# Expert stage: spare rows in four buffers, asked for three quads ahead, and a later start for the weights of experts 6 and up

## What is computed

```python
C = int(math.ceil(CAPACITY_FACTOR * T / E))          # 1.25 * 4096 / 32 = 160
top1 = jnp.argmax(probs, axis=-1)
pos = jnp.cumsum(onehot, axis=0)[jnp.arange(T), top1] - 1
accepted = pos < C
buf = jnp.zeros((E * C + 1, H)).at[slot].set(xt)
g = jnp.einsum('ech,ehf->ecf', buf, w_gate)
u = jnp.einsum('ech,ehf->ecf', buf, w_up)
y = jnp.einsum('ecf,efh->ech', jax.nn.silu(g) * u, w_down)
return (xt + out_tok).reshape(B, S, H)               # out_tok: the token's row of y, times its gate
```

## Time and profile before

| | us |
|---|---|
| median of 3 runs | 3612.1 |
| these runs | 3604.91 to 3613.67 |
| the profiled execution's own time | 3612.02 |
| its span in the profile | 3610.2 |

### The profile page before, as it was taken

One profiled execution on the slowest core, in us unless ns is written; L12 is line 12 of the kernel. 1 busy time (PEld: TensorE's weight loads), 2 busy tenths in 40 slices (PEclk: granted clock), 3 DMA queues, 4 the chain that ended last, 5 costly groups with the idle time before them and its releaser, 6 DMA issues. The chain is left out here.

```text
span 3610.2 us, 52197 instructions
## 1 busy us (share of the span) xinstructions
PE 3197.4 (89%) x18048; PEld 1971.1 (55%) x18048; DVE 2459.1 (68%) x4614; ACT 1846.4 (51%) x3942; POOL 1413.2 (39%) x967
## 2 busy tenths in 40 slices
PE   8599999979999799899999899898388888887867
PEld 5244444346666555566666555333255556555766
DVE  8488887657767622277777332498799999996623
ACT  2176776836666511166666211356477777774100
POOL 4201111132222211132222211234699999996612
PEclk9699999989999899999999899999699999999888
DMA  5945576010020033000200131244615151512874
GB/s 168 164 63 90 78 97 125 28 38 24 23 62 25 29 151 98 26 23 23 63 25 19 56 96 47 72 152 149 241 59 205 59 205 59 204 59 73 294 232 143
DMA packets 263747, 347.27 MB, mean 96 GB/s; under 512 B 70620, under 2 KB 183242, under 8 KB 262845
## 3 DMA queue, kind: packets, MB, share of 16 engines
q1 hardware_dynamic: 249572, 308.29, 30.7%
q10 hardware_dynamic: 9432, 23.35, 2.0%
q0 software_dynamic: 4480, 12.30, 0.9%
HBM read 227.72 MB, written 112.80 MB: 94 GB/s over the span
## 5 line engine op out<-in xcount | busy, mean ns | idle before, releaser
L2411 POOL TENSOR_TENSOR H_feed<-H_ndu,H_bs 128x1024 f32<-128x1024 f32 x256 | 595.1, 2367 | 5.3 <-DMA H_cs<-between_bc 3.1
L888 ACT ACTIVATE B_probs<-B_p_exp,B_key_bias 128x512 f32<-128x512 f32 (+3 forms) x768 | 394.1, 582 | 159.7 <-PE B_p_exp L950 129.2
L779 DVE TENSOR_REDUCE B_part_max<-B_p_max 128x1 f32<-128x512 f32 (+3 forms) x768 | 374.5, 545 | 78.7 <-PE B_p_max L914 76.2
L1298 ACT ACTIVATE D_probs<-D_scores,D_neg,D_rq 128x256 f32<-128x256 f32 x512 | 282.9, 574 | 255.4 <-DVE D_neg L1219 255.4
L2382 ACT ACTIVATE H_decay<-H_ndt,H_rate 128x1024 f32<-128x1024 f32 x256 | 287.7, 1125 | 199.0 <-DVE H_turning L2464 103.3
L1662 PE MATMUL E_p_ag<-E_hT,FA_w 128*128 128x512 f32 x640 | 284.1, 603 | 1.9 <-ACT E_hT L1618 1.9
L911 PE MATMUL B_p_max<-B_k,B_q 100*128 100x512 bf16 (+3 forms) x768 | 256.3, 340 | 30.0 <-DMA B_q<-in_q_rows 20.1
L947 PE MATMUL B_p_exp<-B_q,B_k 100*128 100x512 bf16 (+3 forms) x768 | 249.6, 329 | 23.1 <-DMA B_q<-B_shift_rows 16.2
L2464 DVE TENSOR_TENSOR_SCAN H_turning<-H_decay,H_feed 128x1024 f32<-128x1024 f32 x112 | 253.5, 2274 | 20.2 <-POOL H_feed L2411 17.4
L2515 PEld LDWEIGHTS H_p_y<-H_minus,H_sT 128*128 128x128 f32 x1792 | 222.4, 198 | 75.9 <-ACT H_sT L2367 56.1
L2515 PE MATMUL H_p_y<-H_minus,H_sT 128*128 128x128 f32 x1792 | 230.9, 285 | 35.7 <-ACT H_sT L2367 35.7
(11 more groups left out here) (276 smaller groups left out, 6812.3 us busy)
## 6 DMA issues: line engine op xcount, KB each, us to landing
H_bs<-between_bc SPq DMA_DIRECT2D x64, 512.0 KB, 7.3
H_cs<-between_bc SPq DMA_DIRECT2D x36, 512.0 KB, 7.6
B_q<-between_q_parts SPq DMA_DIRECT2D x90, 128.0 KB
B_k<-between_k_parts SPq DMA_DIRECT2D x90, 128.0 KB
between_slots_x<-E_clear ACTq DMA_DIRECT2D x4, 2570.0 KB, 18.8
I_xe<-between_slots_x ACTq DMA_DIRECT2D x32, 257.0 KB, 3.0
LA_base<-between_z SPq DMA_DIRECT2D x64, 128.0 KB, 2.2
between_z<-D_z SPq DMA_DIRECT2D x64, 128.0 KB
```

The costliest lines, as they stand in the source:

```text
L779: nc.vector.reduce_max(part_max[:, g % 2, kc, qb, h:h + 1], p_max[:, use % 3, 0:keys], AX.X).then_inc(maxed, 1)
L888: nc.scalar.activation(probs[:, x % PROBS, skip:512], p_exp[:, n % SCORES, skip:512], ACT.Exp, bias=key_bias[:, g % SETS, kb - 4 * Q + 4, ...
L1298: last = nc.scalar.activation(probs[:, place[m], :, :].rearrange("p a b -> p (a b)"), scores[:, place[m], :, :].rearrange("p a b -> p (a b ...
L2411: nc.gpsimd.tensor_tensor(feed[:, n % AHEAD, :], ndu[:, g % 2, :], bs[:, s, :], ALU.mult).then_inc(fed, 1)
```

## The change

`xr`, `token_rest` and the semaphores `xr_loaded` get four buffers. ACT asks for the spare rows of quads 1, 2 and 3 right after the first six experts' rows, and from then on for those of quad `e // QUAD + 3` at the second expert of a quad; the last such request is that for quad 7 at expert 17. `tokens_rest(f)` waits for the return of quad f - 4, since that one used the same list. SP gets seven waits ahead of the weights of expert 6: for the spare rows of quad 0 and for the rows of experts 0 to 5. The order of the work on PE and DVE stays as it is.

```diff
-        QUAD, HR = 4, 8
+        QUAD, HR, XR = 4, 8, 4
-        token_rest = a.sb("token_rest", [P, 2, 1], I32)
+        token_rest = a.sb("token_rest", [P, XR, 1], I32)
-        xr = a.sb("xr", [P, 2, ROW])
+        xr = a.sb("xr", [P, XR, ROW])
-        xr_loaded = [a.sem(f"xr_loaded_{b}") for b in range(2)]
+        xr_loaded = [a.sem(f"xr_loaded_{b}") for b in range(XR)]
@@ SP @@
             for c in range(K - 2, K):
                 store_sums(c)
+            sp.wait_ge(xr_loaded[0], 16 * QUAD)
+            for b in range(XE - 2):
+                sp.wait_ge(xe_loaded[b], 16)
             for e in range(K - 2, EXPERTS):
                 load_weights(e)
@@ DVE @@
             def tokens_rest(f):
-                dve.wait_ge(xr_loaded[f % 2], 16 * QUAD * (f // 2 + 1))
-                reached(dve, rest_returned[f % 2], 16 * (f // 2))
-                nc.vector.tensor_scalar(token_rest[:, f % 2, :], xr[:, f % 2, TOKEN:TOKEN + 1], -1.0, float(TOKENS),
+                dve.wait_ge(xr_loaded[f % XR], 16 * QUAD * (f // XR + 1))
+                if f >= XR:
+                    dve.wait_ge(rest_returned[f % 2], 16 * ((f - XR) // 2 + 1))
+                nc.vector.tensor_scalar(token_rest[:, f % XR, :], xr[:, f % XR, TOKEN:TOKEN + 1], -1.0, float(TOKENS),
@@ ACT @@
             def load_rests(f):
-                if f >= 2:
-                    act.wait_ge(xe_turned, (f - 2) * QUAD + 1)
-                    act.wait_ge(y_ready, rest_use(f - 2) + 1)
-                    act.wait_ge(rest_tokens_ready, f - 1)
+                if f >= XR:
+                    act.wait_ge(xe_turned, (f - XR) * QUAD + 1)
+                    act.wait_ge(y_ready, rest_use(f - XR) + 1)
+                    act.wait_ge(rest_tokens_ready, f - XR + 1)
...
-            load_rests(1)
+            for f in range(1, XR):
+                load_rests(f)
...
-                if e % QUAD == 1 and QUAD <= e < EXPERTS - QUAD:
-                    load_rests(e // QUAD + 1)
+                if e % QUAD == 1 and QUAD <= e < EXPERTS - (XR - 1) * QUAD:
+                    load_rests(e // QUAD + XR - 1)
```

More of the change, by code:

```diff
@@ L2764, in _ @@
                     pool.wait_ge(rest_tokens_ready, f + 1)
-                    pool.indirect_dma_start(T["out"][:, :], bass.IndirectOffsetOnAxis(token_rest[:, f % 2, :], axis=0),
+                    pool.indirect_dma_start(T["out"][:, :], bass.IndirectOffsetOnAxis(token_rest[:, f % XR, :], axis=0),
                                             y_rest[:, f % 2, :], None, bounds_check=TOKENS - 1, oob_is_err=False
@@ L2878, in put_y_rest @@
                 reached(dve, rest_returned[f % 2], 16 * (f // 2))
-                nc.vector.scalar_tensor_tensor(y_rest[:, f % 2, :], p_y[:, rest_use(f) % 2, :], xr[:, f % 2, GATE:GATE + 1],
-                                               xr[:, f % 2, SUM], ALU.mult, ALU.add).then_inc(y_ready, 1)
+                nc.vector.scalar_tensor_tensor(y_rest[:, f % 2, :], p_y[:, rest_use(f) % 2, :], xr[:, f % XR, GATE:GATE + 1],
+                                               xr[:, f % XR, SUM], ALU.mult, ALU.add).then_inc(y_ready, 1)
             def tokens(e):
@@ L2938, in load_rests @@
             def load_rests(f):
-                if f >= 2:
-                    act.wait_ge(xe_turned, (f - 2) * QUAD + 1)
-                    act.wait_ge(y_ready, rest_use(f - 2) + 1)
-                    act.wait_ge(rest_tokens_ready, f - 1)
+                if f >= XR:
+                    act.wait_ge(xe_turned, (f - XR) * QUAD + 1)
+                    act.wait_ge(y_ready, rest_use(f - XR) + 1)
+                    act.wait_ge(rest_tokens_ready, f - XR + 1)
                 for j in range(QUAD):
                     at = (f * QUAD + j) * CAPACITY + P
-                    act.dma_start(xr[REST * j:REST * j + REST, f % 2, :], T["slots_x"][at:at + REST, :]
-                                  ).then_inc(xr_loaded[f % 2], 16)
+                    act.dma_start(xr[REST * j:REST * j + REST, f % XR, :], T["slots_x"][at:at + REST, :]
+                                  ).then_inc(xr_loaded[f % XR], 16)
             def put_xT(c):
@@ L3026, in turn_rows @@
                 if e % QUAD == 0:
-                    pe.wait_ge(xr_loaded[f % 2], 16 * QUAD * (f // 2 + 1))
+                    pe.wait_ge(xr_loaded[f % XR], 16 * QUAD * (f // XR + 1))
                     for k in range(KD):
                         nc.tensor.transpose(p_xr[:, k, :, :].rearrange("p j n -> p (j n)"),
-                                            xr[:, f % 2, k:DIM:KD], ident[:, :])
+                                            xr[:, f % XR, k:DIM:KD], ident[:, :])
                 for k in range(KD):
```

## The result

| | before | after |
|---|---|---|
| median of 5 runs, us | 3610.99 | 3572.2 |
| these runs | 3604.91 to 3613.67 | 3567.76 to 3576.65 |
| the profiled execution's own time | 3612.02 | 3574.62 |
| its span | 3610.2 | 3572.8 |

The ratio is 0.9892, 95% interval 0.9882 to 0.9903: 38.8 us less, against 40.8 forecast (3571.2, range 3562 to 3588).

A forecast was written before the change was run, and what follows sets the result against it. The prediction took PE to bound the stage of experts, interrupted by the late `xr` transfer. From 3612.0 us it took 36.4 for the advance and 4.4 for the hold, giving 3571.2 us, range 3562 to 3588.

The forecast's parts named there:

- What bounds the stage: Stage of experts: PE bounds it, interrupted by the `xr` transfer asked for one loop pass before it is read.
- rival D: Stage of experts: PE's stall has another cause, earlier requests move only the label; time 3608, chance 0.03.
- (1) Advance: -36.4: Six quad periods: three quads of advance remove the stalls, 123.15 us falls to 86.8, and nothing is late next.
- (2) DMA capacity: Stage of experts: DMA work exceeds PE's 14.46 us a quad, piling up about 1 us for each of five quads.
- rival B: Stage of experts: DMA engines become the bound if bytes take some 3% longer; time 3576 to 3586, chance 0.18.
- The rule set against a row: DMA rate: the skill's 358 GB/s gives 14.1 us for a period's bytes, the row 15.9; the prediction took the row.
- (3) The hold: -4.4: Stage start: with weights of experts 6 to 11 held, the last scatter lands in 3.2 us, 4.4 earlier (0 to 5.3).
- (4) ACT's requests: Before the first Silu: eight more DMAs slip it 2.0 us within 3.7 us of slack; cost 0, up to 1.5.
- Sum: Whole kernel: 3612.0 - 36.4 - 4.4 = 3571.2 us; bounds of the parts give 3570.3 to 3577.1.
- C: DVE's `tokens(e)`: the return of `y` takes the stall's place if landings exceed 10 us; 3583 to 3601, chance 0.10.
- E: Stage of experts: slower than before through DMA load, needing a rate of 225 GB/s; 3638 at 0.6, chance 0.03.
- weights landed in more than 13 us: Sign in the changed profile: weights land in over 13 us at DMA share near 1, PE never waiting for them.

The follow-up runs named there:

- no_late_weights: Kernel before without loading the weights of experts 12 to 31, which use what lies in the ring (wrong results): 3578.15 us, ratio 0.9908.
- burst_behind_rows: Kernel before plus SP's seven waits, each burst of weights for a quad also waiting until the previous quad's spare rows landed: 3582.98 us, ratio 0.9921.
- buffers_only: Changed kernel without SP's seven waits, four buffers and three quads of advance kept: 3580.58 us, ratio 0.9904.
- extra_one: Changed kernel plus one 256 KB DRAM to DRAM DMA behind each expert's weights from expert 6 on: 3565.4 us, ratio 0.9874.
- hold_until_scattered: Changed kernel with SP waiting for the scatters of the routing instead of the rows: 3572.09 us, ratio 0.9887.
- hold_only: Kernel before plus SP's seven waits alone, two buffers for the spare rows: 3606.61 us, ratio 0.9987.
- extra_two: Changed kernel plus two 256 KB DRAM to DRAM DMAs behind each expert's weights from expert 6 on: 3586.76 us, ratio 0.9936.
- three_warm_short: Changed kernel with three buffers, quad 2's request behind the first Silu and 13 matmuls without use on PE before the first transposes: 3570.57 us, ratio 0.9882.

## Why the prediction was right, step by step

- **What bounds the stage.** PE, interrupted by the transfer of `xr`: right. But the price was put on lateness alone, although rival D cites the last period, in which no weights are asked for and there is no stall. no_late_weights shows that the late request costs 2.9 us of the 36.1 by itself, and with burst_behind_rows that the burst of weights beside it is what lengthens the landing until PE also loses its clock.
- **(1) Advance: -36.4.** The free quad of 14.46 us measured 14.50 to 14.51. The six periods went from 123.15 to 87.03 us, 36.1 less; buffers_only gives 37.5 for the stage. The term is right to 1 us. That nothing is late next holds as well.
- **(2) DMA capacity.** This is the step with a wrong size. It set 15.1 to 15.9 us of DMA work (length times share) for a quad against 14.46 us, and so found a pile of 5 us, 9 with the held weights. In the kernel after the share falls to 0.99 in the fourth window, which a growing pile would not allow, and the engines caught up soon after the last request for weights, which is at 3527.30 (after, columns as above):

```profile
3536.00:3538.00 2.00, 2.00 (x17) 1.97 (x16) 0.23 (x1) 0.44 (x1) 1.58 (x2) 1.00 0.51 107
3538.00:3542.00 4.00, 4.00 (x28) 3.85 (x27) 2.16 (x8) 0.44 (x1) 0.98 (x1) 1.00 0.24 87
```

  Two sizes were off. The share of engines that never rest is 1.04 or 1.05 and not 1, so a window of 14.5 us can hold 15.2 us of such work. And GB/s over share went from 318 to 332 in the four rows of before to 333 to 369 after, and 358 to 375 in extra_one. Gaps are not what made the rate of before low; inside its bursts, with the engines full, it is some 320 GB/s too:

```profile
3509.00:3519.00 10.00, 4.93 (x32) 4.63 (x32) 1.92 (x6) 0.63 (x2) 1.97 (x2) 0.94 1.01 325
3530.50:3540.50 10.00, 5.10 (x32) 4.71 (x31) 2.10 (x7) 0.44 (x1) 1.70 (x2) 0.88 1.01 323
```

  Why the kernel after moves more bytes for the same share stays open. Nothing of the sum hung on this step, but the point at which rival B begins did: by the prediction at 3% less rate; in fact one extra DMA for each expert, a third more weight traffic, was still free.
- **The rule set against a row.** The prediction set the Trainium skill's figure from "DMA: Bandwidth & Descriptors", section Specifications, about 358 GB/s as the HBM limit of a core, against the row with 235 GB/s over a share of 0.74, and went by the row. By that figure nothing would pile up, which came nearer to what happened than my pile did. It is not a ceiling here, though: windows of 387 (after) and 394 GB/s (extra_one) lie above it.
- **(3) The hold: -4.4.** The last scatter landed in 3.22 us (3.2 taken), the first transpose came 4.8 us earlier from that scatter's issue. The change's stage is 3.6 us shorter than buffers_only's. That it protects the first rows too, 2.6 us by hold_until_scattered, the prediction didn't say; it counted only the scatter. The Trainium skill's section "Anatomy of one DMA" on the same page would give 2.6 us for the scatter, an estimate from its formula; nine chains have 2.9 to 3.2 us where no weights run beside it, and three with weights beside it 6.7 to 7.6.
- **(4) ACT's requests.** Predicted slip of Silu 2.0 us, measured 3.0 (from ACT's first request to Silu 12.7 against 9.7 us): twelve requests took 6.39 us instead of 5.3. That SP issues at the same time is not the reason: in buffers_only, where SP issued nothing between 3434.4 and ACT's last of them, the same twelve, from 3447.65 on, took 6.53. What stretches them stays open. The slack was smaller than the 3.7 us of the prediction by about 0.9: the first transposes started 0.4 us sooner behind ACT's first request, and PE needed 0.5 us less from there to the first `reduce`. So a cost of 0 became 0.33 us, within the bound of 1.5.
- **Sum.** 40.8 us predicted, 41.1 in the stage, 38.8 by medians. That it is so close is in part luck: the long scatter alone varied by 0.9 us from one kernel to the next, and the -4.4 us are 3.6 against buffers_only and 6.7 in hold_only.
- **Rivals.** D is refuted by the windows. B and C are real mechanisms and lie outside this kernel's working point, B by two extra DMAs for each expert, C by half the buffers. E did not occur. Whether weights landed in more than 13 us, as the prediction expected, the trace of the kernel after doesn't tell; in extra_one `wd` landed in 12.9 us in the median and 15.3 at most.

## What to carry to other kernels

When an engine waits for a transfer, look at two things before buying buffers: how early it is asked for, and which burst is asked for at the same time; here the same late request landed in 1.9 to 2.6 us without the weights and in 5.8 to 7.2 beside them, and one buffer more was enough. A prefetch that is not needed yet can be held with a semaphore until the transfer that everyone waits for has landed, if its own deadline is far. And measure DMA capacity by adding load, as extra_one and extra_two do: the rate per share read from the kernel before, even from its full windows, was lower than what the changed kernel reached.

## What the hardware did that I had not expected

- With the engines never idle the median landing doubled (results to `out` 2.9 to 5.8 us, `xe` 3.0 to 6.4) while the longest fell (7.5 to 6.4 and to 6.8). In these two traces steady load was kinder to the tail than bursts.
- A rate of 376 to 394 GB/s held for six windows of 14.5 us in a row (extra_one), with reads of weights, rows of 2 KB, scatters and DRAM copies mixed.
- The granted clock stayed at 1.00 through idle times of up to 2.4 us once in a quad (burst_behind_rows), and fell to 0.57 in the 3 us behind one of 1.83 us (extra_two) and to 0.63 behind 1.66 and 0.50 us at the start of the stage (three_warm_short). No run shows what decides.
